# Selective scan with a post-norm: output projection, residual and centring in one PSUM sum, variance from ScalarE

## The chip, the cores and the metric

The kernel runs on one core of one Trainium2 chip. The metric is the device time of one launch in microseconds, as the median of several runs. Engines are called by the names that the profile uses: PE (TensorE; PEld its weight loads), DVE (VectorE), ACT (ScalarE), POOL (GpSimd), SP (SyncE, which only issues transfers here).

## The reference, cut to what matters

Two transformer-like blocks on x of shape 16 x 256 x 128, with a layer norm without weights after each of four sublayers. Only the first sublayer, a selective scan, is touched:

```
x_in = inp - mean(inp)
x, z = split(x_in @ W_in)              # 256 columns each
u = silu(conv4(x) + conv_b)            # depthwise, 4 taps in time
B, C = split(u @ W_x)                  # 16 states each
delta = softplus(u @ W_dt + b_dt)
h = exp(delta * A) * h + delta * B * u # for each channel and state
y = (sum over states of C * h) + u * D
out = (y * silu(z)) @ W_out + inp
x = layernorm(x + out)                 # x + out = 2 * inp + (...) @ W_out
```

The other three sublayers (a small feed-forward net with 4-bit quantising, differential attention, and a three-layer net with weights of plus and minus one) follow and are the same in both kernels.

## The kernel before

The input stays in SBUF as `x_all`, 32 tiles of 128 tokens x 128 features. `mamba_phase` treats it in 8 groups (`GROUPS`) of 4 tiles (`GT`), 512 tokens, which are two sequences. Channels lie on the partitions, in two chunks `c` of 128. A group has 32 units `i`: state `s = i // 2`, chunk `c = i % 2`. For each unit:

- ACT, `decays`: exp(delta * A) into one of four PSUM banks `dA`. Before unit `i` it waits until DVE has left the bank that unit `i - 4` used, and mostly clears two start columns first (L469), then does the exponential (L472).
- POOL, `drive`: delta * u * B for two units at once into `dBu`, 8 units deep.
- DVE, `scan`: the recurrence over time (L334). Its result times C goes to `hC`: on DVE (`times_c`, L343) for 23 units of the 32, on POOL (L544) for the other 9, four units later in POOL's program.
- PE, `accumulate`: adds `hC` into the PSUM bank `yac` of its chunk, as a matmul with the identity (L582).

Every engine runs its own program, a hand-written order in which the unit number says where other work is put in. While group `n` is scanned, the projections of group `n + 1` are made in two PSUM banks `pp` (`step` on PE and on ACT: transposed input at unit 26 of the group ahead, convolution at 0 and 2, B and C at 8, delta at 10 and 12, its softplus on ACT at 16 to 21 and 23, z at 19 and 21), and group `n - 1` is finished:

- DVE at unit 2, `leave`: `yac` times the gate gives `yg`.
- PE at unit 16, `project_out`: for each of 4 tiles two matmuls `yg` x `w_out` into bank `pp[1]`.
- DVE at unit 21, `residual`: r = 2 * x + `pp[1]` (L360). DVE at unit 23, `stat`: mean and variance of each row (L109, L112, L114).
- POOL at unit 29, `shifts`: four tiny operations that make `rstd` and `shift` = -mean * rstd.
- ACT at unit 4 of the group after, `normalize`: r * rstd + shift back into `x_all` (L479).

A DVE, ACT or POOL instruction that waits on a semaphore holds back all that stands behind it in its engine's program. The weights W_in are centred once at the start, by a matmul with `center` = identity - 1/128, so x needs no centring of its own.

Of the kernel before, what the change touches and what calls it, by code (L numbers as in the profile page):

```python
# [13 lines left out]
ALU = mybir.AluOpType  # L14
# [7 lines left out]
P = 128  # L22
# [36 lines left out]
EARLY_N = MAMBA_N + FFN_N + (2 + QB) * (FFN_N // QB) + (2 + 4 * QB) * X_BLOCKS  # L59
LATE_N = 12800  # L60
LAMBDA_INIT = 0.8 - 0.6 * math.exp(-0.3 * 12)
# [130 lines left out]
def mamba_phase(nc, k):  # L192
# [11 lines left out]
    with ctx:  # L204
# [16 lines left out]

        center = sb("center", [P, P])
        wk = sb("wk", [P, TAPS, DI])
        wz = sb("wz", [P, DI])
        diag = sb("diag", [P, CH, P])
        xT = sb("xT", [P, 2, SEQ + 3])
        zraw = sb("zraw", [P, CH, GTOK])
# [12 lines left out]
        yg = sb("yg", [P, CH, GTOK])  # L240
        r = sb("r", [P, GT, P])
        stats = sb("stats", [P, GT, 6])
        mv = sb("mv", [P, GT, 2])
        veps = sb("veps", [P, GT])
        rstd = sb("rstd", [P, GT])
        nmean = sb("nmean", [P, GT])
        shift = sb("shift", [P, GT])
        spare = sb("spare", [P, 1])
        eps = sb("eps", [P, GT])
        minus = sb("minus", [P, GT])  # L250
        zero = sb("zero", [P, 2, 1])
# [36 lines left out]
        out_ready = sem("out_ready")  # L288
        r_ready = sem("r_ready")
        stat_chain = sem("stat_chain")  # L290
        shift_ready = sem("shift_ready")
        norm_chain = sem("norm_chain")
# [29 lines left out]
        def _(dve):  # L322
# [33 lines left out]

            def residual(m):
                dve.wait_ge(out_ready, m + 1)
                wait(dve, norm_chain, m)
                nc.vector.scalar_tensor_tensor(  # L360
                    out=r[:].rearrange("p a b -> p (a b)"),
                    in0=k.x_all[:, GT * m:GT * m + GT, :].rearrange("p a b -> p (a b)"), scalar=2.0,
                    in1=pp[1][:], op0=ALU.mult, op1=ALU.add).then_inc(r_ready, 1)

            def stat(m):
                dve.wait_ge(r_ready, m + 1)
                wait(dve, shift_ready, m)
                layer_norm_stats(dve, nc, r, stats, mv, spare, stat_chain, 2 * m)

            nc.vector.memset(xT[:], 0.0).then_inc(zeros_ready, 1)  # L370
# [21 lines left out]
            for n in range(GROUPS + 1):  # L392
                for i in range(UNITS):
                    if n < GROUPS:
                        scan(n, i)
                        if i and not POOL_C[i - 1]:
                            times_c(n, i - 1)
                    if i == 2 and n >= 1:
                        leave(n - 1)
                        if n == GROUPS:  # L400
                            quant_scale(nc, dve, k, k.qx, ffn_blocks(k, 0), 0)
                            quant_abs(nc, dve, k.qx, 0)
                            quant_magic(nc, dve, k.qx, 0)
                    if i == 21 and n >= 1:
                        residual(n - 1)
                    if i == 23 and n >= 1:
                        stat(n - 1)
                    if i in (27, 28) and n + 1 < GROUPS:
                        drive_factor(n + 1, i - 27)
                if n < GROUPS and not POOL_C[UNITS - 1]:  # L410
                    times_c(n, UNITS - 1)
# [3 lines left out]
        def _(act):  # L415
            def took_xT(m):
                act.wait_ge(x_turned, m + 1)
                nc.scalar.activation(xT[:, :, 1:SEQ + 1], pp[0][:].rearrange("p (a b) -> p a b", a=2),
                                     ACT.Copy).then_inc(xT_ready, 1)
# [41 lines left out]
            def decays(n, i):  # L461
# [8 lines left out]
                else:  # L470
# [3 lines left out]
                                     ACT.Exp, scale=decay[:, NS * c + s:NS * c + s + 1]).then_inc(decay_ready, 1)  # L474

            def normalize(m):
                act.wait_ge(shift_ready, m + 1)
                for j in range(GT):
                    last = nc.scalar.activation(k.x_all[:, GT * m + j, :], r[:, j, :], ACT.Identity,  # L479
                                                scale=rstd[:, j:j + 1], bias=shift[:, j:j + 1])  # L480
                last.then_inc(norm_chain, 1)

            def step(m, i):

                if i == 10:
                    silus(m)
                if i == 14:
                    took_bc(m)
                if 16 <= i < 22:
                    softplus(m, (i - 16) // 3, (i - 16) % 3)  # L490
                if i == 23:
                    log(m)
                if i == 25:
                    took_z(m, 0)
                if i == 28:
                    took_z(m, 1)
                if i == 31 and m + 1 < GROUPS:
                    took_xT(m + 1)
# [4 lines left out]
            act.wait_ge(wcent_done, 1)  # L503
            nc.scalar.activation(wz[:], pp[1][:, DI:2 * DI], ACT.Copy).then_inc(wz_ready, 1)
            act.wait_ge(zeros_ready, 2 + RA)
            for i in range(UNITS):
                step(0, i)
            for n in range(GROUPS):
                for i in range(UNITS):
                    decays(n, i)  # L510
                    if n + 1 < GROUPS:
                        step(n + 1, i)
                    if i == 6:
                        gates(n)
                    if i == 4 and n >= 2:
                        normalize(n - 2)
            normalize(GROUPS - 2)
            normalize(GROUPS - 1)

        @block.gpsimd  # L520
        def _(pool):
# [24 lines left out]

            def shifts(m):
                pool.wait_ge(stat_chain, 2 * m + 2)
                nc.gpsimd.tensor_tensor(veps[:], mv[:, :, 1], eps[:], ALU.add).then_inc(rstd_step, 1)
                nc.gpsimd.tensor_tensor(nmean[:], mv[:, :, 0], minus[:], ALU.mult).then_inc(rstd_step, 1)  # L550
                pool.wait_ge(rstd_step, 3 * m + 1)
                wait(pool, norm_chain, m)
                nc.gpsimd.tensor_tensor(rstd[:], veps[:], k.neg_half[:, 0:GT], ALU.pow).then_inc(rstd_step, 1)
                pool.wait_ge(rstd_step, 3 * m + 3)
                nc.gpsimd.tensor_tensor(shift[:], nmean[:], rstd[:], ALU.mult).then_inc(shift_ready, 1)

            nc.gpsimd.memset(k.neg_half[:], -0.5).then_inc(half_ready, 1)
            nc.gpsimd.memset(eps[:], LN_EPS).then_inc(half_ready, 1)
            nc.gpsimd.memset(minus[:], -1.0).then_inc(half_ready, 1)
            pool.wait_ge(half_ready, 3)  # L560
            quant_middle(nc, pool, k.qw, 0)
# [3 lines left out]
            for n in range(GROUPS + 1):  # L565
                for i in range(UNITS):
# [7 lines left out]
                    if n == GROUPS and i == 28:  # L574
                        quant_middle(nc, pool, k.qx, 0)
                    if i == 29 and n >= 1:
                        shifts(n - 1)

        @block.tensor
        def _(pe):  # L580
# [9 lines left out]
            def conv(m, c):  # L590

                pe.wait_ge(xT_ready, m + 1)
                wait(pe, z_took, CH * m)
                for t in range(TAPS):
                    last = mm(pp[c][:], wk[:, t, P * c:P * c + P], xT[:, :, t:t + SEQ], t == 0, t == TAPS - 1)
                last.then_inc(conv_done, 1)

            def z_proj(m, c):
                if c == 0:
                    pe.wait_ge(sp_step, 7 * m + 5)  # L600
                else:
                    pe.wait_ge(sp_step, 7 * m + 2)
                    wait(pe, r_ready, m - 1)
                mm(pp[c][:], wz[:, P * c:P * c + P], xT[:, :, 1:SEQ + 1]).then_inc(z_done, 1)

# [15 lines left out]
            def accumulate(n, i):  # L621
# [6 lines left out]
                if s == 0:  # L628
                    wait(pe, y_step, CH * (n - 1) + c + 1)
                if i in (SKIP_AT, SKIP_AT + 1):  # L630
                    mm(yac[c][:], diag[:, c], u[:, n % 2, c], False, False)
                mm(yac[c][:], ident, hC[:, g % RH], s == 0, s == NS - 1).then_inc(acc_done, 1)

            def project_out(m):
                pe.wait_ge(y_step, CH * m + CH)
                pe.wait_ge(sp_step, 7 * min(m + 2, GROUPS - 1) + 2)
                for j in range(GT):
                    for c in range(CH):
                        last = mm(pp[1][:, P * j:P * j + P], yg[:, c, P * j:P * j + P],
                                  w_out[:, P * c:P * c + P], c == 0, c == CH - 1)  # L640
                last.then_inc(out_ready, 1)

            def step(m, i):
# [11 lines left out]
                if i == 19:  # L655
                    z_proj(m, 0)
                if i == 21:
                    z_proj(m, 1)
# [7 lines left out]
            pe.wait_ge(center_ready, 1)  # L666
            mm(pp[1][:], center[:], w_in).then_inc(wcent_done, 1)
            pe.wait_ge(wk_ready, TAPS)
            pe.wait_ge(wz_ready, 1)
# [1211 lines left out]
def build(nc, io, out):  # L1881
    ctx = ExitStack()
    with ctx:
# [8 lines left out]
        k.ident = sb("ident", [P, P])  # L1892
        k.identb = sb("identb", [P, P], BF16)


# [177 lines left out]
```

## Time and the profile before

| | us |
|---|---|
| median of 3 runs (lowest, highest) | 1156.83 (1154.6, 1157.79) |
| the profiled execution, its own time | 1154.77 |
| its span, from first to last instruction | 1152.9 |
| scan phase, groups 0 to 7 and the end of the last | about 41 to 506 |
| busy in the span: PE, DVE, ACT, POOL | 940.9, 938.7, 718.9, 826.7 |

Times of rows are microseconds from the start of the span. What lies around the span is 1.9 us. TensorE's granted clock has a mean of 0.921 of full over the span.

### The profile page before, as it was taken

What the parts mean: (1) busy time and instruction counts of PE and PEld (TensorE: products, weight loads), DVE (VectorE), ACT (ScalarE), POOL (GpSimd) and SP (SyncE); (2) the same over time, 40 slices, a digit from 0 to 9 for tenths busy, and PEclk for the clock granted to TensorE, in tenths of its full rate; (3) what the DMA queues carried; (4) which work ended last, traced back from release to release, by engine and by line L of the source; (5) the groups of instructions that cost most, each with busy time, mean ns of one, the idle gap of its engine ahead of it and who ended that gap; (6) DMA issues with size and microseconds to landing.
All of it is one profiled execution on the core that took longest, in us unless ns stands there. A gap on an engine that the chain in (4) does not pass through costs nothing. (4 is left out here: it accounts for less than half of the span.)

```text
span 1152.9 us, 15456 instructions
## 1 busy us (share of the span) xinstructions
PE 940.9 (82%) x4332; PEld 471.9 (41%) x4347; DVE 938.7 (81%) x1597; ACT 718.9 (62%) x1406; POOL 826.7 (72%) x771
## 2 busy tenths in 40 slices
PE   6697979898989796757777457999999998599995
PEld 2233334333333342334455333455555543355453
DVE  3699999999999999958875236788888885469996
ACT  2785767677777675423444224777777767588772
POOL 1798999999999999827555564577787833677773
PEclk9799999998999998988887675999999999799998
DMA  4651515251525151032000032322323310000000
GB/s 143 288 222 73 221 73 221 73 222 73 222 73 221 73 221 73 1 81 50 1 1 1 0 92 87 98 83 87 112 77 89 113 57 2 1 1 10 19 18 29
DMA packets 34877, 103.84 MB, mean 90 GB/s; under 512 B 3627, under 2 KB 22443, under 8 KB 23979
## 3 DMA queue, kind: packets, MB, share of 16 engines
q1 hardware_dynamic: 34807, 103.03, 25.9%
q8 instruction: 30, 0.49, 0.2%
q14 instruction: 40, 0.33, 0.1%
HBM read 93.71 MB, written 8.91 MB: 89 GB/s over the span
## 5 line engine op out<-in xcount | busy, mean ns | idle before, releaser
L582 PE MATMUL m_yac<-m_hC,ident 128*128 128x512 f32 x512 | 267.1, 642 | 73.2 <-DVE m_hC L343 47.0
L534 POOL TENSOR_TENSOR m_dBu<-m_du,m_Bt 128x1024 f32<-128x1024 f32 x128 | 299.5, 2358 | 8.2 <-DVE m_dA L334 6.8
L334 DVE TENSOR_TENSOR_SCAN m_dA<-m_dA,m_dBu 128x512 f32<-128x512 f32 x184 | 221.6, 1218 | 15.0 <-ACT m_dA L472 12.1
L1235 DVE TENSOR_REDUCE a_nm<-bank 128x2 f32<-128x512 f32 x256 | 169.0, 683 | 41.7 <-PE bank L1474 40.9
L1422 ACT ACTIVATE late<-bank 128x512 f32<-128x512 f32 x256 | 151.5, 602 | 77.0 <-PE bank L1474 75.9
L582 PEld LDWEIGHTS m_yac<-m_hC,ident 128*128 128x128 f32 x512 | 93.3, 198 | 226.3 <-issue 105.8
L472 ACT ACTIVATE m_dA<-m_delta,early 128x510 f32<-128x510 f32 x256 | 169.2, 674 | 0.3
L343 DVE TENSOR_TENSOR m_hC<-m_dA,m_Ct 128x512 f32<-128x512 f32 x184 | 123.0, 669 | 0.0
L1474 PE MATMUL bank<-ks,qs 72*128 72x256 bf16 x512 | 102.8, 285 | 22.6 <-DVE a_nm L1235 13.2
L544 POOL TENSOR_TENSOR m_hC<-m_hS,m_Ct 128x512 f32<-128x512 f32 x72 | 94.2, 1308 | 31.7 <-DVE m_hS L334 31.5
L469 ACT ACTIVATE m_dA<-m_zero 128x2 f32<-128x2 f32 x181 | 30.8, 170 | 127.7 <-DVE m_hC L343 127.4
L1474 PE MATMUL bank<-qs,ks 99*128 99x256 bf16 x512 | 100.1, 278 | 4.1 <-ACT late L1422 2.4
L334 DVE TENSOR_TENSOR_SCAN m_hS<-m_dA,m_dBu 128x512 f32<-128x512 f32 x72 | 86.7, 1205 | 0.0
L1813 PE MATMUL bank<-qs,early 128*128 128x512 bf16 x375 | 84.7, 379 | 0.5
L1474 PEld LDWEIGHTS bank<-qs,ks 99*128 99x128 bf16 x512 | 44.3, 99 | 65.4 <-ACT late L1422 47.7
L1474 PE MATMUL bank<-late,vx 128*32 128x512 f32 x512 | 69.0, 613 | 0.0
L1474 PEld LDWEIGHTS bank<-ks,qs 72*128 72x128 bf16 x512 | 44.2, 100 | 52.2 <-DVE a_nm L1235 34.2
L582 PE MATMUL m_pp<-m_xT,m_wk 128*128 128x512 f32 x128 | 63.4, 642 | 2.1 <-DVE m_wk L379 2.1
L1765 POOL TENSOR_TENSOR ks<-ks 128x512 f32<-128x512 f32 x32 | 38.6, 1208 | 28.8 <-ACT ks L1789 21.4
L1813 PEld LDWEIGHTS bank<-qs,early 128*128 128x128 bf16 x384 | 36.8, 98 | 44.9 <-issue 1.9
L1402 POOL TENSOR_TENSOR a_rms<-a_ms_eps,neg_half 128x16 f32<-128x16 f32 x16 | 47.8, 2984 | 1.2
L1765 POOL TENSOR_TENSOR qs<-qs 128x512 f32<-128x512 f32 x32 | 38.7, 1216 | 12.0 <-ACT qs L1789 11.2
(219 smaller groups left out, 1820.1 us busy)
## 6 DMA issues: line engine op xcount, KB each, us to landing
m_Bt<-bcd SPq DMA_DIRECT2D x32, 1024.0 KB, 6.0
m_Ct<-bcd SPq DMA_DIRECT2D x32, 1024.0 KB, 6.6
qs<-parts SPq DMA_DIRECT2D x16, 576.0 KB
ks<-parts SPq DMA_DIRECT2D x48, 192.0 KB
parts<-a_part SPq DMA_DIRECT2D x32, 192.0 KB, 2.2
out<-x_all SPq DMA_DIRECT2D x8, 256.0 KB, 2.3
early<-in_mprm SPq DMA_DIRECT2D x1, 1203.0 KB, 6.7
vx<-in_vrow SPq DMA_DIRECT2D x4, 256.0 KB
```

The source lines that it names most:

```text
L334: nc.vector.tensor_tensor_scan(out, decay, dBu[:, g % RD], 0.0, ALU.mult, ALU.add).then_inc(scan_ready, 1)
L343: nc.vector.tensor_tensor(hC[:, g % RH], dA[g % RA][:].rearrange("p a b -> p (a b)"), Ct[:, s], ALU.mult).then_inc(hcd_ready, 1)
L472: nc.scalar.activation(dA[g % RA][:, :, 1:SEQ], delta[:, n % 2, c].rearrange("p (a b) -> p a b", a=2)[:, :, 1:SEQ], ACT.Exp, scale=decay[: ...
L534: nc.gpsimd.tensor_tensor(dBu[:, g % RD:g % RD + CH], du[:, n % 2], Bt[:, s].unsqueeze(1).broadcast_to([P, CH, GTOK]), ALU.mult).then_inc( ...
L544: nc.gpsimd.tensor_tensor(hC[:, g % RH], hS[:, on_pool(n, i) % RS], Ct[:, s], ALU.mult).then_inc(hcp_ready, 1)
L582: return nc.tensor.matmul(out, lhsT, rhs, start=start, stop=stop)
L1235: nc.vector.tensor_reduce(nm[:, slot % 2, q, 2 * pair:2 * pair + 2], s1[i % 2][:], AX.X, ALU.max, negate=True).then_inc(max_ready, 1)
L1402: nc.gpsimd.tensor_tensor(rms[:], ms_eps[:], k.neg_half[:, 0:TS * NH], ALU.pow).then_inc(rms_chain, 1)
L1422: nc.scalar.activation(pT[:, u // 2, u % 2], s2[u % 2][:], ACT.Exp, scale=float(HD) ** -0.25).then_inc(exp_ready, 1)
L1474: return nc.tensor.matmul(out, lhsT, rhs, start=start, stop=stop)
L1765: nc.gpsimd.tensor_tensor(rest_tile(s, c), full_tile(s, c), part_tile(s, q, c, 0), ALU.subtract).then_inc(s.rest_ready, 1)
L1813: return nc.tensor.matmul(out, lhsT, rhs, start=start, stop=stop)
```

## The change

- The input weights' centring matrix is also applied to `w_out`, once at the start, and the result is halved: `wo` = center x W_out / 2. Host code hands over `w_out` transposed.
- `project_out` adds the input to the same PSUM sum: for each of 4 tiles one matmul of the transposed input `xT` with `center`, then the two of `yg` x `wo`. The bank then holds half of the centred row of 2x + y W_out. For this `xT` is kept for three groups instead of one.
- DVE's `residual` and `stat` go. ACT does `squares` at unit 19: four Square activations with a sum along the row, straight from PSUM. POOL does `rstds` at unit 24, two tiny operations in place of four. ACT does `normalize` at unit 26 of the same group, from PSUM, with the scale alone.
- Because `pp[1]` is now held until `normalize`, the second half of the z projection moves on PE from unit 21 to 27, and its copy on ACT from unit 28 to 30.

```diff
-        xT = sb("xT", [P, 2, SEQ + 3])
+        xT = sb("xT", [P, 3, 2, SEQ + 3])
...
-                    if i == 21 and n >= 1:
-                        residual(n - 1)
-                    if i == 23 and n >= 1:
-                        stat(n - 1)
...
+            def squares(m):
+                act.wait_ge(out_ready, m + 1)
+                wait(act, rstd_ready, m)
+                for j in range(GT):
+                    last = nc.scalar.activation(k.x_all[:, GT * m + j, :], pp[1][:, P * j:P * j + P], ACT.Square,
+                                                scale=DM ** -0.5, accum_out=var[:, j:j + 1])
+                last.then_inc(var_ready, 1)
+
             def normalize(m):
-                act.wait_ge(shift_ready, m + 1)
+                act.wait_ge(rstd_ready, m + 1)
                 for j in range(GT):
-                    last = nc.scalar.activation(k.x_all[:, GT * m + j, :], r[:, j, :], ACT.Identity,
-                                                scale=rstd[:, j:j + 1], bias=shift[:, j:j + 1])
+                    last = nc.scalar.activation(k.x_all[:, GT * m + j, :], pp[1][:, P * j:P * j + P], ACT.Copy,
+                                                scale=rstd[:, j:j + 1])
                 last.then_inc(norm_chain, 1)
...
-                if i == 28:
+                if i == 30:
                     took_z(m, 1)
...
+            act.wait_ge(wo_done, 1)
+            nc.scalar.activation(wo[:], yac[0][:, 0:CH * DM].rearrange("p (c d) -> p c d", c=CH),
+                                 ACT.Copy, scale=0.5).then_inc(wo_ready, 1)
...
-                    if i == 4 and n >= 2:
-                        normalize(n - 2)
-            normalize(GROUPS - 2)
+                    if i == 19 and n >= 1:
+                        squares(n - 1)
+                    if i == 26 and n >= 1:
+                        normalize(n - 1)
+            squares(GROUPS - 1)
             normalize(GROUPS - 1)
...
+            def rstds(m):
+                pool.wait_ge(var_ready, m + 1)
+                nc.gpsimd.tensor_tensor(veps[:], var[:], eps[:], ALU.add).then_inc(rstd_step, 1)
+                pool.wait_ge(rstd_step, m + 1)
                 wait(pool, norm_chain, m)
+                nc.gpsimd.tensor_tensor(rstd[:], veps[:], k.neg_half[:, 0:GT], ALU.pow).then_inc(rstd_ready, 1)
...
-                    if i == 29 and n >= 1:
-                        shifts(n - 1)
+                    if i == 24 and n >= 1:
+                        rstds(n - 1)
...
                     pe.wait_ge(sp_step, 7 * m + 2)
-                    wait(pe, r_ready, m - 1)
+                    wait(pe, norm_chain, m - 1)
...
                 for j in range(GT):
+                    a, b = divmod(P * j, SEQ)
+                    mm(pp[1][:, P * j:P * j + P], xT[:, m % 3, a, b + 1:b + 1 + P], center[:], True, False)
                     for c in range(CH):
-                        last = mm(pp[1][:, P * j:P * j + P], yg[:, c, P * j:P * j + P],
-                                  w_out[:, P * c:P * c + P], c == 0, c == CH - 1)
+                        last = mm(pp[1][:, P * j:P * j + P], yg[:, c, P * j:P * j + P], wo[:, c], False, c == CH - 1)
...
-                if i == 21:
+                if i == 27:
                     z_proj(m, 1)
...
+            for c in range(CH):
+                last = mm(yac[0][:, DM * c:DM * c + DM], w_out[:, P * c:P * c + P], center[:])
+            last.then_inc(wo_done, 1)
```

## Rows read from the trace of the kernel before

**Rows 1.** Waits up to 460 us: who waited for whom, total, times, longest.

```profile
ACT m_dA L469 <- DVE m_hC L343: 112.2, 104, 5.0
...
DVE m_dA L334 <- ACT m_dA L472: 12.1, 15, 0.9
```

**Rows 2.** Timeline of DVE, group 4: start, length, instruction, idle before.

```profile
301.94 2.34 DVE L334 TENSOR_TENSOR_SCAN m_dA<-m_dA,m_dBu 128x512 f32<-128x512 f32 x2
...
304.77 0.67 DVE L360 SCALAR_TENSOR_TENSOR m_r<-x_all,m_pp 128x512 f32<-128x512 f32 x1
305.36 1.23 DVE L334 TENSOR_TENSOR_SCAN m_dA<-m_dA,m_dBu 128x512 f32<-128x512 f32 x1
...
308.80 0.86 DVE L109 BATCH_NORM_STATS2 m_stats<-m_r 128x6 f32<-128x128 f32 x4
...
310.17 2.34 DVE L334 TENSOR_TENSOR_SCAN m_dA<-m_dA,m_dBu 128x512 f32<-128x512 f32 x2
...
329.28 1.26 DVE L355 TENSOR_TENSOR m_yg<-m_yac,m_gate 128x512 f32<-128x512 f32 x2
```

**Rows 3.** Timeline of PE, group 4, from one `leave` to the next.

```profile
272.96 1.10 PE L582 MATMUL m_yac<-m_hC,ident 128*128 128x512 f32 x2 [1.28 <-DVE m_yg L355]
...
301.68 1.95 PE L582 MATMUL m_pp<-early,m_yg 128*128 128x128 f32 x16
303.46 2.74 PE L582 MATMUL m_yac<-m_hC,ident 128*128 128x512 f32 x6
...
319.71 1.12 PE L582 MATMUL m_yac<-m_hC,ident 128*128 128x512 f32 x2 [1.58 <-POOL m_hC L544]
...
330.10 1.10 PE L582 MATMUL m_yac<-m_hC,ident 128*128 128x512 f32 x2 [2.54 <-DVE m_yg L355]
```

**Rows 4.** Timeline of ACT, group 4, units 19 to 25.

```profile
298.24 0.67 ACT L449 ACTIVATE m_sp_r<-m_pp,early 128x512 f32<-128x512 f32 x1
299.23 0.18 ACT L469 ACTIVATE m_dA<-m_zero 128x2 f32<-128x2 f32 x1 [0.32 <-DVE m_hC L343]
...
303.46 1.28 ACT L458 ACT_TABLE_LOAD   x1
...
307.80 0.15 ACT L469 ACTIVATE m_dA<-m_zero 128x2 f32<-128x2 f32 x1
```

**Rows 5.** Groups of ACT instructions: busy us, mean ns of one, idle before.

```profile
L479 ACT ACTIVATE x_all<-m_r,m_shift,m_rstd 128x128 f32<-128x128 f32 x32 | 13.1, 478 | 14.0 <-POOL m_shift L555 14.0
...
L1459 ACT ACTIVATE late<-late 128x256 f32<-128x256 f32 x16 | 6.5, 409 | 0.3 <-DVE late L1270 0.3
...
L934 ACT ACTIVATE late<-bank 128x128 f32<-128x128 f32 x2 | 0.4, 274 | 0.2 <-PE bank L977 0.2
```

**Rows 6.** Timeline of POOL, group 4.

```profile
303.47 4.68 POOL L534 TENSOR_TENSOR m_dBu<-m_du,m_Bt 128x1024 f32<-128x1024 f32 x2
...
314.39 1.01 POOL L553 TENSOR_TENSOR m_rstd<-m_veps,neg_half 128x4 f32<-128x4 f32 x1
```

**Rows 7.** Timeline of PE, group 2: `leave` and projection.

```profile
158.68 2.05 PE L582 MATMUL m_yac<-m_hC,ident 128*128 128x512 f32 x2 [2.65 <-DVE m_yg L355]
...
188.99 1.95 PE L582 MATMUL m_pp<-early,m_yg 128*128 128x128 f32 x16
```

**Rows 8.** Windows of PE: length, busy (instructions), granted clock, DMA share, GB/s.

```profile
160.00:164.00 4.00, 4.00 (x8) 0.76 0.00 0
164.00:168.00 4.00, 4.00 (x10) 1.00 0.00 0
```

**Rows 9.** Timelines of PE and DVE, group 7, the last.

```profile
470.61 1.95 PE L582 MATMUL m_pp<-early,m_yg 128*128 128x128 f32 x16
```
```profile
472.32 2.34 DVE L334 TENSOR_TENSOR_SCAN m_dA<-m_dA,m_dBu 128x512 f32<-128x512 f32 x2
```

**Rows 10.** Timeline of all engines, after the last scan.

```profile
496.59 2.05 PE L582 MATMUL m_pp<-early,m_yg 128*128 128x128 f32 x16 [1.38 <-DVE m_yg L355]
...
501.03 1.26 POOL L179 TENSOR_TENSOR early<-early 128x512 f32<-128x512 f32 x1
...
503.88 1.65 ACT L479 ACTIVATE x_all<-m_r,m_shift,m_rstd 128x128 f32<-128x128 f32 x4 [13.98 <-POOL m_shift L555]
```

**Rows 11.** Timeline of all engines, before the first scan.

```profile
4.64 0.49 DVE L370 MEMSET m_xT<- 128x518 f32 x1 [4.64 <-PEq L1912]
...
11.18 1.42 DVE L379 TENSOR_TENSOR m_wk<-m_pp,early 128x256 f32<-128x256 f32 x4 [3.69 <-ACT m_wz L504]
```

More of the change, by code:

```diff
@@ L59 @@
 EARLY_N = MAMBA_N + FFN_N + (2 + QB) * (FFN_N // QB) + (2 + 4 * QB) * X_BLOCKS
-LATE_N = 12800
+LATE_N = 13056
 LAMBDA_INIT = 0.8 - 0.6 * math.exp(-0.3 * 12)
@@ L220, in mamba_phase @@
         ident = k.ident[:]
-        center = sb("center", [P, P])
+        center = k.center
+        wo = sb("wo", [P, CH, DM])
         wk = sb("wk", [P, TAPS, DI])
@@ L240, in mamba_phase @@
         yg = sb("yg", [P, CH, GTOK])
-        r = sb("r", [P, GT, P])
-        stats = sb("stats", [P, GT, 6])
-        mv = sb("mv", [P, GT, 2])
+        var = sb("var", [P, GT])
         veps = sb("veps", [P, GT])
         rstd = sb("rstd", [P, GT])
-        nmean = sb("nmean", [P, GT])
-        shift = sb("shift", [P, GT])
-        spare = sb("spare", [P, 1])
         eps = sb("eps", [P, GT])
-        minus = sb("minus", [P, GT])
         zero = sb("zero", [P, 2, 1])
@@ L288, in mamba_phase @@
         out_ready = sem("out_ready")
-        r_ready = sem("r_ready")
-        stat_chain = sem("stat_chain")
-        shift_ready = sem("shift_ready")
+        wo_done = sem("wo_done")
+        wo_ready = sem("wo_ready")
+        var_ready = sem("var_ready")
+        rstd_ready = sem("rstd_ready")
         norm_chain = sem("norm_chain")
@@ L355, in leave @@
                     nc.vector.tensor_tensor(yg[:, c], yac[c][:], gate[:, c], ALU.mult).then_inc(y_step, 1)
[L357 to L368, printed above, removed]
             nc.vector.memset(xT[:], 0.0).then_inc(zeros_ready, 1)
@@ L417, in took_xT @@
                 act.wait_ge(x_turned, m + 1)
-                nc.scalar.activation(xT[:, :, 1:SEQ + 1], pp[0][:].rearrange("p (a b) -> p a b", a=2),
+                nc.scalar.activation(xT[:, m % 3, :, 1:SEQ + 1], pp[0][:].rearrange("p (a b) -> p a b", a=2),
                                      ACT.Copy).then_inc(xT_ready, 1)
@@ L545, in times_c @@
                                         ALU.mult).then_inc(hcp_ready, 1)
[L547 to L551, printed above, removed]
+            def rstds(m):
+                pool.wait_ge(var_ready, m + 1)
+                nc.gpsimd.tensor_tensor(veps[:], var[:], eps[:], ALU.add).then_inc(rstd_step, 1)
+                pool.wait_ge(rstd_step, m + 1)
                 wait(pool, norm_chain, m)
-                nc.gpsimd.tensor_tensor(rstd[:], veps[:], k.neg_half[:, 0:GT], ALU.pow).then_inc(rstd_step, 1)
-                pool.wait_ge(rstd_step, 3 * m + 3)
-                nc.gpsimd.tensor_tensor(shift[:], nmean[:], rstd[:], ALU.mult).then_inc(shift_ready, 1)
+                nc.gpsimd.tensor_tensor(rstd[:], veps[:], k.neg_half[:, 0:GT], ALU.pow).then_inc(rstd_ready, 1)
             nc.gpsimd.memset(k.neg_half[:], -0.5).then_inc(half_ready, 1)
-            nc.gpsimd.memset(eps[:], LN_EPS).then_inc(half_ready, 1)
-            nc.gpsimd.memset(minus[:], -1.0).then_inc(half_ready, 1)
-            pool.wait_ge(half_ready, 3)
+            nc.gpsimd.memset(eps[:], LN_EPS / 4).then_inc(half_ready, 1)
+            pool.wait_ge(half_ready, 2)
             quant_middle(nc, pool, k.qw, 0)
@@ L594, in conv @@
                 for t in range(TAPS):
-                    last = mm(pp[c][:], wk[:, t, P * c:P * c + P], xT[:, :, t:t + SEQ], t == 0, t == TAPS - 1)
+                    last = mm(pp[c][:], wk[:, t, P * c:P * c + P], xT[:, m % 3, :, t:t + SEQ], t == 0, t == TAPS - 1)
                 last.then_inc(conv_done, 1)
@@ L602, in z_proj @@
                     pe.wait_ge(sp_step, 7 * m + 2)
-                    wait(pe, r_ready, m - 1)
-                mm(pp[c][:], wz[:, P * c:P * c + P], xT[:, :, 1:SEQ + 1]).then_inc(z_done, 1)
+                    wait(pe, norm_chain, m - 1)
+                mm(pp[c][:], wz[:, P * c:P * c + P], xT[:, m % 3, :, 1:SEQ + 1]).then_inc(z_done, 1)
             def bc_proj(m):
@@ L629, in accumulate @@
                     wait(pe, y_step, CH * (n - 1) + c + 1)
+                    if n == 0 and c == 0:
+                        pe.wait_ge(wo_ready, 1)
                 if i in (SKIP_AT, SKIP_AT + 1):
@@ L636, in project_out @@
                 pe.wait_ge(sp_step, 7 * min(m + 2, GROUPS - 1) + 2)
+                pe.wait_ge(wo_ready, 1)
                 for j in range(GT):
+                    a, b = divmod(P * j, SEQ)
+                    mm(pp[1][:, P * j:P * j + P], xT[:, m % 3, a, b + 1:b + 1 + P], center[:], True, False)
                     for c in range(CH):
-                        last = mm(pp[1][:, P * j:P * j + P], yg[:, c, P * j:P * j + P],
-                                  w_out[:, P * c:P * c + P], c == 0, c == CH - 1)
+                        last = mm(pp[1][:, P * j:P * j + P], yg[:, c, P * j:P * j + P], wo[:, c], False, c == CH - 1)
                 last.then_inc(out_ready, 1)
@@ L1893, in build @@
         k.identb = sb("identb", [P, P], BF16)
+        k.center = sb("center", [P, P])
         k.early = Arena(sb("early", [P, EARLY_N])[:])
@@ L2016 @@
         "w_dt": chunks(i[m + "W_dt"]),
-        "w_out": chunks(i[m + "W_out"]),
+        "w_out": i[m + "W_out"].T,
         "conv_r": np.tile(i[m + "conv_w"].reshape(1, TAPS * DI), (P, 1)),
```

## Prediction

> **What bounds the kernel now.** I read the page first: PE and DVE are both busy for a little over 80% of the span, which names no bound, because the four sublayers have different limits. The change touches only the scan phase, so I read that phase by its waits. Up to 460 us ACT waits 112.2 us for DVE in front of its exponentials, while DVE waits for ACT only 12.1 us in 15 places [rows 1]. So DVE sets the pace of the scan: it goes from scan to product to scan with no gap, and ACT, at most four units ahead, is let on by it. A group takes 57.1 us (330.10 less 272.96, the same point of two groups [rows 3]).
>
> Then I laid the timelines of the engines side by side for group 4, and the thing to see is that PE is a different case. From `leave` at 272.96 it works without a gap to the output projection at 301.68 [rows 3]: 17 accumulations, the two of the skip term, the convolution, B, C and delta of the next group. That is 28.7 us of its own work, and here PE is late: it comes to the projection of unit 16 only when DVE is at unit 20 (301.94 [rows 2]). ACT is early: it has ended its work of unit 19 at about 298.9 [rows 4]. In the kernel before, nobody minds, since the only one who waits for the projection is DVE at unit 21, and it gets there at 304.77 [rows 2] when the projection has ended at 303.6. The change gives this late result to the early engine.
>
> **What is removed.** DVE's residual takes from 304.77 to 305.36, 0.59 us, and its statistics from 308.80 to 310.17, 1.37 us [rows 2]. This is on the path: 1.96 us for each of groups 1 to 7, 13.7 us in all. If nothing else changed, that would be the gain, plus about a microsecond at the end. POOL loses two tiny operations of a group, worth nothing while DVE sets the pace. The old normalisation in ACT at unit 4 goes too; ACT waits for DVE just after it, so it gives back nothing.
>
> **What is added to PE.** 16 projection instructions start at 301.68 and the next thing at 303.46 [rows 3], 0.111 us apiece. Four more matmuls are 8 more instructions, since each f32 matmul shows as two: 24 x 0.111 = 2.67 us, and 0.17 us for the last to end (1.95 less 1.78). The bank is ready at 301.68 + 2.67 + 0.17 = 304.5.
>
> **The new wait of ACT.** `squares` stands in ACT's queue behind unit 19. ACT gets there at 298.9 and is held to 304.5, 5.6 us. Behind it are the exponentials of unit 20 and after, for which DVE waits, and the rest of the softplus, for which z's first half (PE) and delta (POOL) wait.
>
> The four squares: the trace has no activation that sums along a row. From below, a 128x128 activation from PSUM with constant scale is 274 ns [rows 5], perhaps 0.09 us less when they overlap: 0.75 us for four. From above, the old normalisation with two per-row operands is 478 ns: 1.9 us for four. I take 1.1, four of the first, because that has the shape and the source. Squares need no table load: the 16 of attention stand among exponentials and show 409 ns and no load beside them [rows 5].
>
> By the Trainium skill, page "ScalarE: Activation LUTs", section "What ACT_TABLE_LOAD costs", an activation with constant scale and bias is 186 ns and 0.833 ns an element, less some 93 ns of overlap; that estimate gives 0.8 us for the four and would take 2 us off the sum. No row here shows what the accumulator output adds, and the page gives no price for it, so I stay with 1.1.
>
> So: squares end at 305.6; clearing and exponential of unit 20 take 0.72 us more (the softplus step behind it starts at 299.95, 0.72 after 299.23); scan 20 can start at 306.4, where it started at 301.94 [rows 2]. **DVE loses 4.5 us there.**
>
> **The wait that follows.** ACT is now late also for its logarithm at unit 23, with two table loads. From unit 20 to that load it is 299.23 to 303.46 less 0.3 of waiting, 3.9 us, and from the load to the end of the exponential of unit 24 it is 303.46 to 307.80, 4.3 us [rows 4]. Unit 24 is ready at 305.6 + 8.2 = 313.8. DVE, from scan 20 at 306.4, needs 301.94 to 308.80 less the residual, 6.3 us [rows 2], and is there at 312.7: 1.1 us of new waiting. Scan 24 starts at 313.8 in place of 310.17. Each of these groups is 3.6 us longer: 4.5 + 1.1 - 0.59 - 1.37.
>
> From there on ACT has room. `normalize` at unit 26 costs it between 1.1 and 1.9 us (the same two rows); with 1.5, unit 27 is ready at 313.8 + 0.7 + 0.5 + 0.7 + 1.5 + 0.6 = 317.8, and DVE wants it 4.6 us after 313.8, at 318.4. Half a microsecond covers it; at the upper end it is still just covered. POOL's `rstds` comes after the drive that starts at 303.47 and the second of the pair would follow; it waits for the squares a few tenths only, and the power, 1.01 us [rows 6], is over long before ACT asks. POOL waits for delta 2 us or so, which its lead of two drives hides.
>
> **The moved z projection.** At PE's unit 27 it stands behind a product that POOL makes late: 319.71 [rows 3]. Its copy, at ACT's unit 30, will hold ACT by some 4 us until about 322. The exponential of unit 31 is then ready at 322.6 and DVE scans 31 at 323.6. The cover is one microsecond; I cost it at nothing. If TensorE is at half clock there, z takes 0.9 us longer and the cover is all but gone; beyond that each group would pay what exceeds it.
>
> **The clock.** In two of the six groups the road from `leave` to projection takes 30.3 us in place of 28.7: group 2 from 158.68 to 188.99 [rows 7]. TensorE had idled in front of `leave`, and the granted clock in 160 to 164 is 0.76, a mean of the 1.2 and 2.4 GHz levels, before it is 1.00 again [rows 8]. DVE paid nothing for it before; now it pays all of it through ACT: 2 x 1.6 = 3.2 us.
>
> **Group 7** has no projections of a next group. Its output projection starts at 470.61 [rows 9], ends at 473.4, squares and exponential bring 475.3, and scan 20 stood at 472.32: +3.0 less 1.96 gives +1.0. Group 0 has no squares: nothing.
>
> **The ends.** Before the first scan the memset of `xT` is three times as long, 1 us more than 0.49, and the weight product and its copy are new; DVE waits 3.69 us there for another cause [rows 11], and PE and ACT have gaps as long: 0. After the last scan: projection from 496.59, squares to 500.6, variance to 501.8, normalisation to 503.3; POOL's two quantising steps, of which the second began at 501.03, now stand behind the variance and end at 504.5. Before, ACT ended at 505.5 [rows 10]. -1.0.
>
> **The sum.** 6 x 3.6 = 21.8; clock 3.2; last group 1.0; end -1.0: +25.0 us. On the profiled execution's 1154.8 that is 1179.8, and it stood 2 us under the median of its runs, so on the median, 1181.8. I say 1181.
>
> **Rivals.**
> - *A, the forecast*: ACT's wait reaches DVE, 1181. Its own range: squares 0.75 to 1.9 give -2.5 to +5.6 over seven groups; the slow clock in none of the groups gives -3.2. 1175 to 1188.
> - *B, slower yet, by the clock.* PE gets some 3 us more idle time in each group before `leave`, and TensorE starts the next stretch at half clock in all six groups, not two: 4 x 1.6 = 6.4 us more, with the upper squares up to 1194. For it: waits of 2.65 us had the slow start [rows 7]; against it: one of 2.54 us, and four groups in six, had none. The Trainium skill, "TensorE: Matmul & The Clock Gate", section "What's actually happening", has the clock fall after an idle stretch; the trace agrees in group 2, and by that rule alone B would be the likelier.
> - *C, faster.* PE would be at its projection early enough that ACT doesn't hold DVE. It decides when the bank is ready by 300.0 (scan 20 at 301.94 less squares, exponential and the hand-over), 4.5 us sooner than worked out. Then the 13.7 us of removed DVE work come out whole: -14.7 with the end, 1142. For it speaks DVE's role as the pace; against it, that the 28.7 us of PE work are without a gap and none of them is removed.
> - *D, no change.* The projection would be 2 us or so later than ACT's bound, so that gain and wait cancel. Nothing in the rows puts it there.
>
> **Numbers.** A 0.68, B 0.23, C 0.05, D 0.02, and 0.02 for something dearer, such as a table load for the squares. The range 1173 to 1194 holds A and B. About 0.3%, 3.5 us, is what a measurement of this kernel can tell from no change. Faster 0.05, same 0.02, slower 0.93.
>
> **What would show it.** In the waits after: ACT `x_all` waiting for PE `m_pp` with about 5.6 us a group; DVE's scan waiting for ACT with some 50 us in place of 12 (6 x 5.6 and 3.0 more); on DVE's timeline a gap of 4.5 us in front of scan 20 and one of 1 us in front of scan 24; a group of 60.7 us between two waits for `yg`. Wrong would be: no gap before scan 20, or a gap before scan 31, which would be the moved z projection.

## The result and the profile after

The changed kernel takes 1179.29 us (median of 4 runs, 1177.67 to 1184.36) against 1155.71 for the kernel before in the same comparison: a ratio of 1.021, 95% interval 1.0174 to 1.0245, or about 24 us more. The forecast was 1181, in a range of 1173 to 1194, and 25.0 us for the profiled execution, whose span grew from 1152.9 to 1177.3, by 24.4.

The engines' rows of the page, after:

```profile
span 1177.3 us, 15567 instructions
## 1 busy us (share of the span) xinstructions
PE 952.2 (81%) x4415; PEld 476.4 (40%) x4415; DVE 926.3 (79%) x1517; ACT 722.6 (61%) x1471; POOL 822.1 (70%) x754
```

DVE has 12 us less to do than before and the kernel is longer; a table of busy time alone would have promised the opposite. The waits up to 485 us show where it went:

```profile
ACT m_dA L448 <- DVE m_hC L339: 79.6, 91, 2.6
...
DVE m_dA L330 <- ACT m_dA L451: 50.7, 28, 6.1
ACT x_all L462 <- PE m_pp L573: 36.4, 6, 6.9
...
ACT m_zraw L402 <- PE m_pp L573: 23.0, 8, 4.8
```

DVE's wait for ACT's exponentials was 12.1 us [rows 1] and is 50.7. The third row is the new one, 36.4 us in six groups: ACT, at its squares, waiting for the output projection. The seventh, in the last group, lies just past this stretch; up to 500 us the row has 41.2 us in 7 waits. The other side of it is the first row: ACT now waits less often for DVE, 79.6 in place of 112.2.

ACT in group 4, from its unit 19 on (start, length, instruction, idle before):

```profile
307.69 0.67 ACT L428 ACTIVATE m_sp_r<-m_pp,early 128x512 f32<-128x512 f32 x1
314.00 0.28 ACT L462 ACTIVATE x_all<-m_pp 128x128 f32<-128x128 f32 x1 [5.65 <-PE m_pp L573]
314.18 0.19 ACT L462 ACTIVATION_READ_ACCUMULATOR x_all<-m_pp 128x1 f32 x1
...
315.02 0.19 ACT L448 ACTIVATE m_dA<-m_zero 128x2 f32<-128x2 f32 x1
...
322.56 0.69 ACT L451 ACTIVATE m_dA<-m_delta,early 128x510 f32<-128x510 f32 x1
```

PE in the same group:

```profile
282.41 1.10 PE L573 MATMUL m_yac<-m_hC,ident 128*128 128x512 f32 x2 [2.30 <-DVE m_yg L351]
...
311.13 0.38 PE L573 MATMUL m_pp<-center,m_xT 128*128 128x128 f32 x2
...
313.36 0.61 PE L573 MATMUL m_pp<-m_wo,m_yg 128*128 128x128 f32 x4
313.80 2.74 PE L573 MATMUL m_yac<-m_hC,ident 128*128 128x512 f32 x6
```

and DVE:

```profile
310.80 0.67 DVE L339 TENSOR_TENSOR m_hC<-m_dA,m_Ct 128x512 f32<-128x512 f32 x1
315.85 2.42 DVE L330 TENSOR_TENSOR_SCAN m_dA<-m_dA,m_dBu 128x512 f32<-128x512 f32 x2 [4.38 <-ACT m_dA L451]
...
323.29 2.35 DVE L330 TENSOR_TENSOR_SCAN m_dA<-m_dA,m_dBu 128x512 f32<-128x512 f32 x2 [1.01 <-ACT m_dA L451]
...
342.13 1.27 DVE L351 TENSOR_TENSOR m_yg<-m_yac,m_gate 128x512 f32<-128x512 f32 x2
```

Read the three together. PE takes 28.7 us from `leave` to the projection (282.41 to 311.13), as it did before (272.96 to 301.68 [rows 3]), and the projection now takes 2.67 us to the next instruction. ACT has ended unit 19 at 308.4 and stands still for 5.65 us. DVE has its product of unit 18 done by 311.5, where nothing stopped it before [rows 2], and waits 4.38 us before scan 20 and 1.01 before scan 24 (4.47 and 1.10 from start to start, since a scan follows the start of a product by 0.58 us where nothing holds it).

The account of the 24.4 us, from the starts of the `yg` rows on DVE (the rows of 329.28 [rows 2] and 342.13 are two of them):

| stretch | before | after | difference | forecast |
|---|---|---|---|---|
| to the first `leave` | 100.72 | 98.31 | -2.4 | 0 |
| groups 1 to 6 | 342.85 | 366.58 | +23.7 | +25.0 |
| group 7 | 51.68 | 52.72 | +1.0 | +1.0 |
| last `leave` to the next phase | 10.9 | 9.8 | -1.1 | -1.0 |
| the other three sublayers, unchanged | 646.8 | 649.9 | +3.1 | 0 |

### The profile page after: what moved, and what is told of

The parts are those of the page before. It is cut to its first block and busy times, and to the rows that moved or that the text cites. A ratio compares the mean times of both kernels' runs of the same rounds, so it can differ in the third digit from the quotient of the medians.

```text
span 1177.3 us, 15567 instructions
## 1 busy us (share of the span) xinstructions
PE 952.2 (81%) x4415; PEld 476.4 (40%) x4415; DVE 926.3 (79%) x1517; ACT 722.6 (61%) x1471; POOL 822.1 (70%) x754
## 5 line engine op out<-in xcount | busy, mean ns | idle before, releaser
L1420 ACT ACTIVATE late<-bank 128x512 f32<-128x512 f32 x256 | 151.2, 601 | 79.6 <-PE bank L1472 78.6
L1397 POOL TENSOR_TENSOR a_ms_eps<-a_ms,a_eps 128x16 f32<-128x16 f32 x16 | 3.5, 220 | 64.4 <-DVE a_ms L1275 64.4
```

Source lines behind the costliest of these rows:

```text
L1420: nc.scalar.activation(pT[:, u // 2, u % 2], s2[u % 2][:], ACT.Exp, scale=float(HD) ** -0.25).then_inc(exp_ready, 1)
```

## The experiments

**The wait alone.** The kernel before, with one line more on ACT. Nothing is computed with it.

```diff
+                    if i == 19 and n >= 1:
+                        act.wait_ge(out_ready, n)
```

> The kernel before, with one line added: ScalarE waits at its unit 19 for the output projection of the group before, and does nothing with it. Theory (the new wait alone is the cost): the projection of group 4 ends at 303.6 in the trace of before, unit 20's exponential is ready at 304.45, DVE wanted it at 301.94: 2.5 us a group in groups 1 to 6, 1.6 more in two of them by TensorE's slow clock, 1.0 in group 7: +19 us (16 to 22). Rival (the squares and their place before the logarithm are the cost, the wait is mostly covered): 0 to +4 us.

Measured: 1172.33 us, ratio 1.0147 (1.0126 to 1.0169), about +17 us. ACT and DVE of this kernel in group 1:

```profile
130.77 0.17 ACT L469 ACTIVATE m_dA<-m_zero 128x2 f32<-128x2 f32 x1 [4.75 <-PE m_pp L584]
```
```profile
131.58 2.42 DVE L334 TENSOR_TENSOR_SCAN m_dA<-m_dA,m_dBu 128x512 f32<-128x512 f32 x2 [2.45 <-ACT m_dA L472]
...
146.16 1.29 DVE L348 TENSOR_TENSOR m_du<-m_delta,m_u 128x512 f32<-128x512 f32 x1
```

One wait, with no work behind it, makes the gap before scan 20: 2.45 us, where 2.5 were worked out. So the rival that made the squares themselves the cost falls. The group is 1.8 us longer, though, and not 2.5 (58.96 against 57.15): the product of delta and u, which took 2.10 us in four of the six groups 1 to 6 of the kernel before, takes 1.29 here. It starts at another point of POOL's drive, and in both kernels it ends some 0.5 us after that drive does (318.54 after 317.98 in group 4 of the kernel before, 147.45 after 146.91 here); that POOL is the cause is read from the timelines, not tried. A shift in time gave 0.8 us back at another place. Two groups are 1.6 us longer than the other four (60.55 and 60.54), as TensorE's slow start had been priced; the granted clock is 0.59 and 0.57 in the four microseconds at the start of each (276 to 280 and 396 to 400 us).

**The same wait, five units later.**

```diff
+                    if i == 24 and n >= 1:
+                        act.wait_ge(out_ready, n)
```

> The kernel before, with the same added wait of ScalarE for the output projection, but at its unit 24. Theory (only the place of the wait costs): ScalarE gets there at 307.9 in the trace of before, the projection ended at 303.6: 0 us (-2 to +2), no gap in front of scan 20. Rival (a wait of ScalarE on the projection costs wherever it stands, since TensorE is late by the load it carries): +5 us or more.

Measured: 0.9994 (0.9973 to 1.0014), no change. Groups 1 to 6 are 57.13 to 57.16 us each, as before. The same wait costs 17 us at one place and nothing at the other.

**A smaller load in front of it.** The changed kernel without the input's part in the projection:

```diff
-                    a, b = divmod(P * j, SEQ)
-                    mm(pp[1][:, P * j:P * j + P], xT[:, m % 3, a, b + 1:b + 1 + P], center[:], True, False)
...
-                        last = mm(pp[1][:, P * j:P * j + P], yg[:, c, P * j:P * j + P], wo[:, c], False, c == CH - 1)
+                        last = mm(pp[1][:, P * j:P * j + P], yg[:, c, P * j:P * j + P], wo[:, c], c == 0, c == CH - 1)
```

> The changed kernel without the four matmuls of the input with center in the output projection (the residual is left out of the result). Theory (the end of the projection sets scan 20 through ScalarE): the bank is ready 0.9 us earlier in each of groups 1 to 7 and at the end: -7 us against the changed kernel, +17 against before. Rival (ScalarE is bound by its own work): 0 to -1 us against the changed kernel, +23 against before.

Measured: 1.0186 (1.0147 to 1.0224) against before, which is +21 us (17 to 26) and doesn't tell the theory's +17 from the rival's +23. The median is 5.3 us under that of the changed kernel, which was measured in another comparison. So the time decides nothing here; the trace does. Its scan 20 of group 1 and the `leave` after it, and the same of the changed kernel:

```profile
132.58 2.42 DVE L330 TENSOR_TENSOR_SCAN m_dA<-m_dA,m_dBu 128x512 f32<-128x512 f32 x2 [3.49 <-ACT m_dA L451]
...
158.85 1.26 DVE L351 TENSOR_TENSOR m_yg<-m_yac,m_gate 128x512 f32<-128x512 f32 x2
```
```profile
132.57 2.42 DVE L330 TENSOR_TENSOR_SCAN m_dA<-m_dA,m_dBu 128x512 f32<-128x512 f32 x2 [4.38 <-ACT m_dA L451]
...
158.84 1.27 DVE L351 TENSOR_TENSOR m_yg<-m_yac,m_gate 128x512 f32<-128x512 f32 x2
```

Groups of this kernel are 59.63 us against 60.53: 0.89 us of TensorE's work taken away shortens the group by 0.9. The last group follows too, 51.82 against 52.72. TensorE, through ACT, sets these groups' length.

**The moved z projection alone**, in the kernel before.

```diff
-                if i == 21:
+                if i == 27:
                     z_proj(m, 1)
...
-                if i == 28:
+                if i == 30:
                     took_z(m, 1)
```

> The kernel before, with the second half of the z projection moved from TensorE's unit 21 to 27 and its copy from ScalarE's unit 28 to 30, nothing else. Theory: ScalarE is held about 4 us a group by the late product, covered by the two products of delta and u on DVE: 0 us (-2.5 to +1.5, the minus if this is what made the first group shorter). Rival (the cover of one microsecond is used up when TensorE's clock is low): +1 us in each of seven groups, +7 us.

Measured: 1.0008 (0.9993 to 1.0022), no change. ACT waits 34.4 us for it in 10 places and DVE hardly notices. Only in group 6 is the cover used up, and there TensorE is slow: the granted clock is 0.61 from 432 to 436 us, and the two instructions of its accumulation take 2.08 us in place of 1.12. That group is 57.90 us, 0.8 longer than the others.

```profile
433.36 2.08 PE L582 MATMUL m_yac<-m_hC,ident 128*128 128x512 f32 x2 [2.01 <-POOL m_hC L544]
```
```profile
438.02 1.22 DVE L334 TENSOR_TENSOR_SCAN m_hS<-m_dA,m_dBu 128x512 f32<-128x512 f32 x1 [0.67 <-ACT m_dA L472]
```

**The weight product at the start alone**, in the kernel before.

```diff
+            for c in range(CH):
+                mm(yac[0][:, DM * c:DM * c + DM], w_out[:, P * c:P * c + P], center[:])
```

> The kernel before, with the two matmuls of center and W_out added at the start, their result unused. In the trace of the changed kernel the first scan starts 1.2 us earlier and the first leave 2.4 us earlier, which the prediction had at nothing. Theory: the extra matmuls raise TensorE's clock earlier in the first convolution, so the first scan starts 1 to 1.5 us earlier: -1 to -2.5 us. Rival (it comes from xT in three copies or from the moved z projection): 0 us.

Measured: 0.9995 (0.9983 to 1.0008), no change, and the first scan starts at 41.51, not before 41.14. My theory for the 2.4 us at the start falls. The 2.4 us have two halves. One, 1.2 us, lies behind the first scan: the product of delta and u in group 0 takes 3.76 us in the profile of before and 2.52 in that of after. It takes 3.73 with the moved z projection and 2.5 in the six other profiles, the kernel before with only the wait or the weight product added among them, so it isn't the change that shortens it. The other half, 1.2 us, lies before the first scan, where the first convolution differs. Its 16 instructions take 10.04 us before and 8.61 after, but 9.67 here with the product and 8.75 in the kernel of the moved z projection without it. That stretch differs between executions: in the kernel before its instructions stand 0.85 us apart up to about 18.7 and 0.43 us after it, and the switch falls at another point in other profiles. The record of the granted clock reads 1.00 there throughout, so it doesn't show why.

**The squares five units later.** The changed kernel with one number changed, chosen by the control above, so that ACT should no longer hold DVE before scan 20. (In TensorE's text two steps also trade places, which leaves the order in which they run as it was.)

```diff
-                    if i == 19 and n >= 1:
+                    if i == 24 and n >= 1:
                         squares(n - 1)
```

> The changed kernel with the squares moved from ScalarE's unit 19 to 24, all else as it is; GpSimd still waits for them at its unit 24. Theory (the wait moves to GpSimd): no gap in front of scan 20, but GpSimd, free at 305.8, is held to 308.9, its drive of units 28 and 29 ends at about 318.6, and DVE, which would want it near 316.5, waits 2 us: a group of about 57.2 us as before, the last group and the end 1.9 and 1.0 us shorter: -2 us against before (-5 to +1). Rival (GpSimd's lead of two drives covers it): a group of 55.3 us, -14 us against before.

Measured: 1.0141 (1.0112 to 1.0169), +16 us, outside what both the theory and the rival gave, and nearer to the changed kernel than to either. POOL, ACT and DVE in its group 4:

```profile
314.09 0.20 POOL L544 TENSOR_TENSOR m_veps<-m_var,m_eps 128x4 f32<-128x4 f32 x1 [3.17 <-ACT x_all L462]
```
```profile
330.18 0.60 ACT L402 ACTIVATE m_zraw<-m_pp 128x512 f32<-128x512 f32 x1 [8.03 <-PE m_pp L573]
```
```profile
317.81 1.23 DVE L330 TENSOR_TENSOR_SCAN m_dA<-m_dA,m_dBu 128x512 f32<-128x512 f32 x1 [1.28 <-POOL m_dBu L529]
...
324.24 1.23 DVE L330 TENSOR_TENSOR_SCAN m_dA<-m_dA,m_dBu 128x512 f32<-128x512 f32 x1 [2.31 <-POOL m_dBu L529]
...
331.39 1.22 DVE L330 TENSOR_TENSOR_SCAN m_hS<-m_dA,m_dBu 128x512 f32<-128x512 f32 x1 [0.97 <-ACT m_dA L451]
```

The wait did move to POOL as expected, but it is passed on three times, not once: to the drive of unit 26 (1.28), which I had left out, to that of unit 28 (2.31), and by POOL's late product of unit 27 to the z projection behind it and so to ACT, which stands 8.03 us and brings unit 31 late (0.97). Four of the groups 1 to 6 are 59.83 us; the other two are 60.73 and 61.62.

**All five places moved.** From the three timelines of the changed kernel I chose a place for each step at which its input is ready and nobody behind it is due.

```diff
-                    if i == 19 and n >= 1:
+                    if i == 27 and n >= 1:
                         squares(n - 1)
-                    if i == 26 and n >= 1:
+                    if i == 30 and n >= 1:
                         normalize(n - 1)
...
-                    if i == 24 and n >= 1:
+                    if i == 28 and n >= 1:
                         rstds(n - 1)
...
-                if i == 27:
-                    z_proj(m, 1)
                 if i == 26 and m + 1 < GROUPS:
                     turn_x(m + 1)
+                if i == 26:
+                    z_proj(m, 1)
...
-                if i == 30:
+                if i == 31:
                     took_z(m, 1)
```

> The changed kernel with five places moved: squares at ScalarE's unit 27, the variance step at GpSimd's 28, the normalisation at ScalarE's 30, the z projection's second half at TensorE's 26 behind the transposes, its copy at ScalarE's 31. Theory (DVE sets the pace once no engine in front of it is held): the 1.96 us removed from DVE come out in each of groups 1 to 7 and 1 us at the end: a group of 55.2 us, -14.5 us against before (-12 to -17), about 1140. Rival (GpSimd or TensorE is the next bound, as both are over 90% busy in a group): a group of 56.5 us or more, -5 us or less.

Measured: 1144.50 us against 1156.03, ratio 0.9902 (0.9879 to 0.9924), about 11.5 us less than the kernel before and 35 less than the change as it was made. That is short of the 12 to 17 us expected, though the interval reaches 14. Its waits up to 480 us, and the two `leave` rows around group 4:

```profile
DVE m_dA L330 <- ACT m_dA L451: 15.0, 16, 2.9
```
```profile
262.66 1.26 DVE L351 TENSOR_TENSOR m_yg<-m_yac,m_gate 128x512 f32<-128x512 f32 x2
...
317.78 1.26 DVE L351 TENSOR_TENSOR m_yg<-m_yac,m_gate 128x512 f32<-128x512 f32 x2
```

A group is 55.12 to 55.15 us, 2.0 less than before: the 1.96 us taken from DVE, now whole. The rival (POOL or PE as the next bound) falls; DVE still sets the pace. Two of its groups begin with TensorE at the low clock as well (granted 0.60 from 97 to 101 us and 0.66 from 373 to 377) and are no longer than the rest, so a slow start costs nothing there. From the first `leave` to the last, groups 1 to 7 are 14.0 us shorter. The span of this profile is 13.0 us shorter than that of before: 3.5 less up to the first `leave`, and 4.4 more from the last `leave` to the end, where it is 657.7 us in that of before, 662.1 here, and 657.1 to 663.0 over all nine profiles. Why the medians differ by 11.5 and not 14 isn't shown; a variation of that size in the unchanged rest is enough for it.

## Why the prediction was right, step by step

- **PE late, ACT early, and the wait between them**: shown. ACT's wait was put at 5.6 us, it is 5.65; the delay of scan 20 at 4.5, it is 4.47. The wait alone makes a gap, five units later it makes none, and with 0.89 us of TensorE's load taken away the group is 0.90 shorter.
- **Eight more projection instructions**: priced at 2.67 us in all, measured 2.67 (313.80 less 311.13).
- **The squares**: priced at 1.1 us between bounds of 0.75 and 1.9. Measured from 314.00 to 315.02, 1.02. No table load appeared. The estimate from the Trainium skill, page "ScalarE: Activation LUTs", section "What ACT_TABLE_LOAD costs", was 0.8 us for the four; the trace shows 1.02, with a read of the accumulator, 207 ns, beside each 0.28 us activation.
- **The logarithm's delay**: 1.1 us, measured 1.10 from start to start. **The removed DVE work**: 1.96, confirmed by the kernel with all places moved (57.15 to 55.14).
- **A group**: 3.6 us longer by the sum, 3.38 by the trace (60.53 less 57.15). The two delays came as forecast (4.47 and 1.10); the 0.26 us between sum and trace is the product of delta and u, 1.84 us after and 2.10 before. I had costed that product as fixed.
- **The clock**: two slow starts of 1.6 us. Two groups, 3 and 6, are 62.22 us, 1.69 longer; behind the `leave` at 219.37 and that at 402.67 the granted clock is 0.57 and 0.60, in part at the 1.2 GHz level. The kernel without the input's matmuls had no slow start in six groups, the one with the added wait had two. The term holds in size, but its number belongs to the execution; that it was two again is luck.
- **Rival B**, a slow start in all six groups, did not come, but the clock itself fell more often than twice. Of the six `leave`s that open groups 1 to 6 of the changed kernel, the granted clock falls near five, at three of them only ahead of `leave`. The group opened at 342.13 is one of these and takes 60.54 us, like the others. What costs is a fall behind `leave`, where TensorE's work without a gap begins. The wait in front of it doesn't tell the two apart: TensorE waited 1.91 and 2.65 us before the two slow starts (220.18 and 403.48), and 2.64 us before the start at 99.13, which was at full clock. Windows of PE (length, busy, granted clock, DMA share, GB/s):

```profile
220.00:224.00 4.00, 3.82 (x5) 0.57 0.07 29
...
336.00:340.00 4.00, 3.41 (x5) 0.57 0.00 0
340.00:344.00 4.00, 2.15 (x6) 1.00 0.75 262
...
404.00:408.00 4.00, 4.00 (x7) 0.60 0.00 0
```

- **Normalisation and z**: the normalisation cost ACT 1.0 us in place of 1.5 and was covered. The z projection was covered too, with the thin place where it had been put, at a slow TensorE.
- **POOL's lead**: that two drives hide its wait for delta holds in the changed kernel (POOL waits 2.43 us there in group 4, DVE nothing). It was not a property of POOL: in the kernel with the squares at unit 24, a hold of 3.17 us a few instructions earlier reached DVE in two places.
- **Start and rest**: costed at nothing, measured -2.4 and +3.1. That they nearly cancel is luck; the stretches that were costed come to +23.6 against 25.0. The code of the rest is the same, and from the last `leave` to the end the nine profiles span 657.1 to 663.0 us, so a difference of 3 us there needs no cause in the change. Of the start, the first `leave` comes at 98.5 to 100.7 in the three profiles with the start of before, and at 96.9 to 99.2 in the four with the changed one: the two overlap. Half of the 2.4 us is the long product in group 0, which other kernels with the start of before don't have. For the other half, the first convolution takes 8.96 to 10.04 us in those three and 7.13 to 8.96 in the four, so something of it may belong to the change. The trials of two of its parts, the weight product and the moved z projection, found no difference in time; the three copies of `xT` were not tried, and it stays open.

The range's upper end was for rival B, the other end for cheap squares and no slow clock (A's own terms give 1176 to 1187, where the prediction wrote 1175 to 1188); C (faster) would have needed the bank 4.5 us sooner, and it came no sooner than worked out.

## What to carry to other kernels

Before work moves to an engine with idle time, ask at which instruction it will wait and what stands behind it: ACT is early here because it feeds the engine that sets the pace, and a wait on a late producer took that lead away in one step. Lay the timelines of producer, waiter and pace-setter side by side and look for a place where the input is ready and the next thing due is far off; here the same operations cost 24 us at one set of places and gain 11 at another. Then follow the next queue as well, since one step moved by itself handed the wait to GpSimd, which passed it on three times.

## What the runs showed of the hardware that I had not expected

- An activation that sums along its row shows as two instructions, 278 ns for 128x128 from PSUM and 207 ns for reading the accumulator; they overlap, and four pairs take 1.02 us.
- TensorE's granted clock fell near five of the six `leave`s that open groups 1 to 6 of the changed kernel, and lengthened only the two groups in which it fell behind `leave`. With the steps at their new places it lengthened none.
- DVE's product of delta and u, whose operands both lie in SBUF, takes 0.67 us where no GpSimd operation is under way and up to 3.76 us where it starts during one on 128x512 or more; it then ends 0.5 to 0.6 us after that operation or, in the longest cases, the next one. In the kernel before the first of each pair took 1.5 to 2.1 us in groups 1 to 6, with the wait added at ACT's unit 19 1.3, and that changed a group's length by up to 0.8 us. It is not so for every GpSimd operation: where it starts during the power on 128x4 (1.02 us), in the kernel with all places moved, it takes 0.68.
- TensorE's first convolution took 7.13 to 10.04 us over the nine profiles, at a granted clock of 1.00 in all of them. The two matmuls placed in front of it by themselves did not shorten it (9.67).
